# A transformer block with experts on one core: feed-forward output as three products of split operands, and the key epsilon as a product

## The reference

```python
def softmax_kernel(x, proj, is_query):
    xp = einsum('bhnd,md->bhnm', x * norm, proj)
    diag = sum(square(x), -1) * 0.5 * norm * norm
    stab = max(xp, -1) if is_query else max(xp, (-1, -2))
    return ratio * (exp(xp - diag - stab) + EPS_K)
...
k_sum = sum(kp, axis=2);  denom = einsum('bhnm,bhm->bhn', qp, k_sum)
ctx = einsum('bhnm,bhnd->bhmd', kp, v)
out = einsum('bhnm,bhmd->bhnd', qp, ctx) / denom[..., None]
x = layer_norm(video + out @ Wo.T + bo, g2, be2)
ff = relu(x @ W1.T + b1) @ W2.T + b2
return layer_norm(x + ff, g3, be3)
```

## Time and profile before

| | before |
|---|---|
| median of 3 runs | 865.91 us |
| profiled execution | 865.57 us |
| its span, first to last instruction | 863.8 us |
| PE busy (matmul) | 717.7 us |
| DVE busy | 610.2 us |
| ACT busy | 436.4 us |
| POOL busy | 358.0 us |

### The profile page before, as it was taken

How to read it: one execution, slowest core, us unless ns; L and a number is a source line. 1 busy time by engine, 2 the same in 40 slices (tenths; PEclk the granted TensorE clock), 3 DMA queues, 4 the chain that set the end, 5 groups by cost and what they waited for, 6 DMA issues and landing times.

```text
span 863.8 us, 15601 instructions
## 1 busy us (share of the span) xinstructions
PE 717.7 (83%) x5761; PEld 580.3 (67%) x5761; DVE 610.2 (71%) x1387; ACT 436.4 (51%) x668; POOL 358.0 (41%) x305
## 2 busy tenths in 40 slices
PE   4778999999999999999999969022469999999930
PEld 3737758768778778788687658021359999888830
DVE  4735837978978978978879664667837666776681
ACT  3544745846746646647557522054044445555461
POOL 4084234525417416515535352200135555555573
PEclk9769999999999999999999979555569999999975
DMA  8000010021021020030110111240043555566494
GB/s 233 2 24 3 2 49 2 1 74 51 2 74 49 24 80 17 24 98 0 49 50 2 65 35 49 74 154 0 7 141 77 130 139 144 146 142 165 123 242 104
DMA packets 51229, 61.51 MB, mean 71 GB/s; under 512 B 9328, under 2 KB 45424, under 8 KB 51184
## 3 DMA queue, kind: packets, MB, share of 16 engines
q1 hardware_dynamic: 42928, 46.98, 16.9%
q0 software_dynamic: 7296, 13.77, 8.2%
q10 hardware_dynamic: 960, 0.17, 0.1%
HBM read 39.80 MB, written 21.10 MB: 71 GB/s over the span
## 4 chain that ended last, share of the span: by engine, by line
PE 71%; DVE 12%; ACT 8%; issue 4%; POOL 3%; DMA 1%; POOLq 0%; ACTq 0%; DVEq 0%
PE pF L1460 11%; PE pX L1460 11%; PE pX L1767 10%; PE pF L1501 7%; PE pA L1460 5%; PE pX L1471 4%; PE pA L1511 4%; ACT kp L506 3%; PE pX L1437 3%; PE pA L1437 3%; PE pA L1452 3%; PE pX L1452 3%; ACT kp L510 2%; DVE qe L1178 2%; PE pX L1543 2%
## 5 line engine op out<-in xcount | busy, mean ns | idle before, releaser
L1501 PE MATMUL pF<-w,h 128*128 128x256 f32 x512 | 120.2, 382 | 0.0
L1501 PEld LDWEIGHTS pF<-w,h 128*128 128x128 f32 x512 | 93.9, 190 | 14.8 <-issue 3.4
L810 POOL DMA_INDIRECT kp<-row_scratch,idx_g x32 | 41.5, 1297 | 128.3 <-issue 67.9
L733 POOL TENSOR_SCALAR ve<-mv 128x4 f32<-128x4 f32 x40 | 9.2, 229 | 206.3 <-DVE mv L891 205.9
L642 ACT ACTIVATE h<-pX,b1cur 128x512 f32<-128x512 f32 x64 | 44.2, 690 | 87.0 <-DVE b1cur L1329 68.7
L1767 PE MATMUL pX<-w_lo,h_hi 128*128 128x256 f32 x256 | 73.2, 286 | 0.8 <-issue 0.8
L1767 PE MATMUL pX<-w_hi,h_lo 128*128 128x256 f32 x256 | 72.4, 283 | 0.0
L1767 PE MATMUL pX<-w_hi,h_hi 128*128 128x256 f32 x256 | 72.4, 283 | 0.0
L474 ACT ACTIVATE h<-pF,b1c 128x512 f32<-128x512 f32 x64 | 44.3, 692 | 40.2 <-PE pF L1460 40.2
L1285 DVE TENSOR_TENSOR h_lo<-h,h_hi 128x512 fp32r<-128x512 f32 x64 | 42.9, 690 | 30.6 <-ACT h_hi L634 30.6
L897 DVE TENSOR_SCALAR z<-z,mv,rstd 128x256 f32<-128x256 f32 x64 | 58.8, 980 | 7.1 <-POOL rstd L735 7.1
(11 more groups left out here) (312 smaller groups left out, 1979.6 us busy)
## 6 DMA issues: line engine op xcount, KB each, us to landing
kp<-fc1T SPq DMA_DIRECT2D x8, 1024.0 KB
w<-fc2T SPq DMA_DIRECT2D x8, 1024.0 KB
xin<-video SPq DMA_DIRECT2D x8, 512.0 KB, 3.7
x<-video SPq DMA_DIRECT2D x8, 512.0 KB, 4.5
out<-x SPq DMA_DIRECT2D x8, 512.0 KB, 2.9
acc_scratch<-xf SPq DMA_DIRECT2D x8, 512.0 KB, 3.0
row_scratch<-y SPq DMA_DIRECT2D x8, 512.0 KB, 3.0
kp<-acc_scratch SPq DMA_DIRECT2D x4, 512.0 KB, 5.6
```

The lines of the kernel that those rows point to most:

```text
L810: pool.indirect_dma_start(xg[:, g, :], None, row_d, bass.IndirectOffsetOnAxis(ap=idx_g[:, g:g + 1], axis=0)).then_inc(gathered, 16)
L1501: ins = nc.tensor.matmul(pF[m][:, half * D:(half + 1) * D], h[:, k, tok(2 * m + half)], w2[:, k, :], start=(k == 0), stop=(k == FC - 1))
```

## The change

1. Feed-forward output. `h` gets a high part `h_hi` (ScalarE copies, new `ff_hi`, two by two among the first four `relu`, then one behind each) and a low part `h_lo` (GpSimd subtracts, new `rest_of_hidden`, eight per batch). `w2` is split once in batch 0: `w2_hi` on ScalarE behind `cs_copy`, `w2_lo` on VectorE ahead of the head masks. `ff_out` makes three float32r products where it made one float32 product. The first call takes all `h_hi` products first and the `h_lo` products last.
2. Key epsilon. `eps_k` goes. The context product gets one more step, the sum of `v` over the tiles (`vsum`, two GpSimd additions) times a constant epsilon, and the sum of keys gets `N * EPS_K` as the bias of `cs_copy`.
3. Order and homes. GpSimd does the eight `rest_of_hidden` ahead of `xnb` and the key sums; scale and shift of `x2` move to the end of its body. `normed(3)` goes from VectorE to ScalarE (`z_norm`, ahead of `exp_q`), with a small product `nz` on VectorE; the other norms use `scalar_tensor_tensor` with the root as a broadcast second input in the place of `tensor_scalar`. VectorE's `ln1_stats` moves ahead of the sum `x1`, `add_ff(0)` behind the norms. The pieces of the last `ff_out` are cut at 4, 5, 7 in place of 4, 6, 7. Buffers share homes: `x2` with `r`, `aT_hi` with `qsq_hi`, `aT_lo` with `qsq_lo`, `cs`, `vsum` and `oT` inside `qe`; the expert loop's `w2e` and the second half of the last sums get homes of their own.

```diff
+            def ff_hi(f, n):
+                act.wait_ge(h_ready, f * FC + n + 1)
+                nc.scalar.activation(h_hi[:, n, :], h[:, n, :], ACT.Copy).then_inc(h_hi_ready, 1)
...
-            def eps_k(i, t):
-                act.wait_ge(ke_ready, i * TT + t + 1)
-                nc.scalar.activation(kp[:, t, :], kp[:, t, :], ACT.Identity, bias=epsk_c[:, 0:1]).then_inc(kp_ready, 1)
...
+            def z_norm(u):
+                act.wait_ge(ny_ready, 2 * u + 1)
+                for t in range(TT):
+                    ins = nc.scalar.activation(z[:, t, :], z[:, t, :], ACT.Identity, bias=nz[:, t:t + 1], scale=rstd[3][:, t:t + 1])
+                ins.then_inc(zf_ready, 1)
...
                 if ff:
                     for n in range(4, FC):
                         relu(f, n)
-                if att:
-                    for t in range(2):
-                        exp_k(i, t)
-                        eps_k(i, t)
+                        ff_hi(f, n)
+                if att:
+                    exp_k(i, 0)
+                    exp_k(i, 1)
                     q_tops(i)
...
+                if ut:
+                    z_norm(u)
...
+                    if isinstance(i, int) and i == 0:
+                        act.wait_ge(wff_in, 16 * N_WFF)
+                        nc.scalar.activation(w2_hi[:], w2[:], ACT.Copy).then_inc(w2_hi_ready, 1)
...
+            def rest_of_hidden(f, n):
+                pool.wait_ge(h_hi_ready, f * FC + n + 1)
+                nc.gpsimd.tensor_tensor(h_lo[:, n, :], h[:, n, :], h_hi[:, n, :].bitcast(F32), ALU.subtract).then_inc(h_lo_ready, 1)
...
+                if i is not None:
+                    pool.wait_ge(v_ready, (i + 1) * 2)
+                    nc.gpsimd.tensor_tensor(vsum, v[:, 0:2], v[:, 2:4], ALU.add).then_inc(vsum_ready, 1)
+                    pool.wait_ge(vsum_ready, 2 * i + 1)
+                    nc.gpsimd.tensor_tensor(vsum[:, 0], vsum[:, 0], vsum[:, 1], ALU.add).then_inc(vsum_ready, 1)
                 if f is not None:
-                    nc.gpsimd.tensor_tensor(x2[:], x2[:], g2_b[:]...
+                    for n in range(FC // 2):
+                        rest_of_hidden(f, n)
                 if u is not None:
                     root(3, u)
                 if f is not None:
-                    nc.gpsimd.tensor_tensor(x2[:], x2[:], b2_b[:]...
+                    for n in range(FC // 2, FC):
+                        rest_of_hidden(f, n)
...
+            def norm_tile(k, t, dst, src):
+                return nc.vector.scalar_tensor_tensor(out=dst[:, t, :], in0=src[:, t, :], scalar=mv[k][:, t, 0:1],
+                                                      in1=rstd[k][:, t:t + 1].to_broadcast([P, D]), op0=ALU.subtract, op1=ALU.mult)
...
+                if isinstance(i, int) and i == 0:
+                    dve.wait_ge(w2_hi_ready, 1)
+                    nc.vector.tensor_tensor(w2_lo[:], w2[:], w2_hi[:].bitcast(F32), ALU.subtract).then_inc(w2_ready, 1)
...
-                        ins = nc.tensor.matmul(pF[m][:, half * D:(half + 1) * D], h[:, k, tok(2 * m + half)], w2[:, k, :],
+                    if m == half == 0:
+                        for k in range(FC):
+                            pe.wait_ge(h_hi_ready, f * FC + k + 1)
+                            nc.tensor.matmul(dst, h_hi[:, k, rows], w2_lo[:, k, :], start=(k == 0), stop=False)
+                            nc.tensor.matmul(dst, h_hi[:, k, rows], w2_hi[:, k, :], start=False, stop=False)
+                        for k in range(FC):
+                            pe.wait_ge(h_lo_ready, f * FC + k + 1)
+                            ins = nc.tensor.matmul(dst, h_lo[:, k, rows], w2_hi[:, k, :], start=False, stop=(k == FC - 1))
+                    else:
+                        for k in range(k0, k1):
+                            for n, (h_, w_) in enumerate(((h_hi, w2_lo), (h_lo, w2_hi), (h_hi, w2_hi))):
...
-                        for t in range(TT):
+                        for t in range(TT + 1):
...
+                                w_, x_ = (v[:, t, cols], kp[:, t, tok(place_of(pair))]) if t < TT else (vsum[:, 0, cols], epsk_c[:, 0:1].to_broadcast([P, P]))
```

More of the change, by code:

```diff
@@ L30 @@
 EPS_K = 1e-4
-N_CONST = 14
+N_CONST = 15
 N_WFF = 13
-N_SEL = 9
+N_SEL = 8
 LN_EPS = 1e-5
@@ L128, in build @@
         w1_lo = sb("w1_lo", [P, C, FF], F32R)
-        w2 = sb("w2", [P, FC, D])
+        with ExitStack() as raw:
+            w2 = raw.enter_context(nc.sbuf_tensor("w2", [P, FC, D], F32))
+        w2_lo = sb("w2_lo", [P, FC, D], F32R)
+        w2_hi = sb("w2_hi", [P, FC, D], F32R)
         gate = sb("gate", [P, C, 32])
@@ L185, in build @@
         gT = sb("gT", [P, P])
-        h = sb("h", [P, FC, N])
+        with ExitStack() as raw:
+            h = raw.enter_context(nc.sbuf_tensor("h", [P, FC, N], F32))
+        h_lo = sb("h_lo", [P, FC, N], F32R)
+        h_hi = sb("h_hi", [P, FC, N], F32R)
         w1_raw = h[:].rearrange("p a b -> p (a b)")[:, 0:C * FF].rearrange("p (c n) -> p c n", c=C)
@@ L277, in build @@
             y = early("y", [P, TT, D])
-        h_hi, h_lo = (sb(n, [P, FC, N], F32R) for n in ("h_hi", "h_lo"))
-        w2_hi, w2_lo = (sb(n, [P, FC, D], F32R) for n in ("w2_hi", "w2_lo"))
-        h_f = h[:].rearrange("p a b -> p (a b)")
-        acc_s = [a.rearrange("p (k t d) -> p k t d", k=LQ, t=TT) for a in (kp_f, h_f)]
+        x2, aT_hi = r, qsq_hi
+        bv_wide = y[:].rearrange("p t d -> p (t d)")[:, 0:C * P].rearrange("p (c n) -> p c n", c=C)
+        w2e = sb("w2e", [P, FC, D])
+        b2cur = sb("b2cur", [P, D])
+        b1e = sb("b1e", [P, E, FC])
+        idm = sb("idm", [P, E, SR, GT])
+        idf = sb("idf", [P, E, GT])
+        Rbd = sb("Rbd", [P, 2, 4, SB], F16)
+        Rbd_be = Rbd[:].rearrange("p k e b -> p k b e")
+        acc_late = sb("acc_late", [P, LQ, TT, D])
+        acc_s = [kp_f.rearrange("p (k t d) -> p k t d", k=LQ, t=TT), acc_late[:]]
         sq_f = sq[:].rearrange("p a b d -> p (a b d)")
@@ L557, in body @@
                     squares(i, 0)
+                if ff:
+                    relu(f, 0)
+                if att:
                     squares(i, 1)
                 if ff:
-                    relu(f, 0)
                     relu(f, 1)
+                    ff_hi(f, 0)
+                    ff_hi(f, 1)
                 if att:
@@ L567, in body @@
                     relu(f, 3)
+                    ff_hi(f, 2)
+                    ff_hi(f, 3)
                 if att:
@@ L1047, in body @@
                 if u is not None:
-                    su.link(normed(3, u, z, z))
+                    dve.wait_ge(rstd_ready[3], u + 1)
+                    nc.vector.scalar_tensor_tensor(out=nz[:], in0=mv[3][:, :, 0], scalar=-1.0, in1=rstd[3][:], op0=ALU.mult,
+                                                   op1=ALU.mult).then_inc(ny_ready, 1)
+                if more:
+                    ln1_stats(i + 1)
+                if u is not None:
+                    dve.wait_ge(zf_ready, u + 1)
                     dve.wait_ge(xres_in, 16 * (u + 1))
@@ L1076, in heads_out @@
                                             rden[:, t, :].unsqueeze(2).to_broadcast([P, H, DH]), ALU.mult).then_inc(at_ready, 1)
-                if f is not None:
-                    add_ff(0)
                 if i is not None:
@@ L1092, in body @@
                     ln1_norm(i + 1)
+                if f is not None:
+                    add_ff(0)
                 if f is not None and i is None:
@@ L1113, in body @@
                     dve.wait_ge(xnb_ready, i + 1)
+                    if f is not None:
+                        dve.wait_ge(z_ready, 2 * (f + 1))
                     for m in range(2):
@@ L1687, in body @@
                     if ff:
-                        ff_out(1, 1, 4, 6)
+                        ff_out(1, 1, 4, 5)
                     pe.wait_ge(oT_ready, (i + 1) * 3)
-                    for t in range(TT):
-                        turn_out(t)
+                    turn_out(0)
+                    turn_out(1)
+                    if ff:
+                        ff_out(1, 1, 5, 7)
+                    turn_out(2)
+                    turn_out(3)
                 if gt_:
@@ L1695, in body @@
                 if att:
-                    if ff:
-                        ff_out(1, 1, 6, 7)
                     pe.wait_ge(at_ready, (i + 1) * TT)
```

110 lines of the change are left out of this document (51 added, 59 removed).

## The result

The changed kernel takes 905.72 us (median of 4 runs, 905.63 to 906.76), the kernel before 865.88 beside it (863.96 to 866.53): ratio 1.0467, interval 1.0449 to 1.0485. It is 40 us slower, where 14 were forecast.

The account below looks back on a forecast made before the run. The prediction took TensorE (PE) to bound the kernel, with the other engines close behind. From 865.57 us, +10.5 for seven bodies, +3.6 for batch 0 and 0 for the end gave 879.7, so 880; range 853 to 891.

Parts of the forecast that it names:

- part 4: Overlap of GpSimd's new work with VectorE's path: four `k_sub` wait 3.4 us a body; called the part that decides.
- the reading part: Share of a GpSimd operation, some 0.7, that a `k_sub` meeting it waits for; scaled from the `wo_lo` row.
- The rival of exclusion for the whole instruction: Each `k_sub` waits until GpSimd's instruction ends: +3.5 us a body, 894 us in all; chance 0.12.
- my +1.5: Net change per steady body: 2.7 + 0.47 - 0.29 - 1.42 = +1.5 us; seven bodies, +10.5 us.
- The drains: The end of the kernel, after the batch bodies: bounded between -2.8 and +2 us, taken as zero.
- one of my signs of being wrong: PE's longest new wait would be at the first `ff_out`, for `h_lo`, which the forecast had just in time.
- Query features: PE's start on them, released by VectorE's `rest_of_tops`, would come 2.7 us later in each body.
- Their second half: Query features' second half: the 2.7 us delay, +0.47 for epsilon products, -0.29 for the old fourth key tile wait.
- the forecast's -1.42: Saving per body from cheaper products in the last two `ff_out` calls: 1.42 us.
- Part 1: Float32r products in `ff_out`: 24 take 2.82 us for 3.53, saving 0.71 us a call, 2.84 us a body.
- Part 5: Batch 0: splitting `w2` ahead of the head masks delays them, +3.6 us, bounds 0 and 6.
- The first rival: No port between VectorE and GpSimd matters, PE is the path: -1.6 us a body, 858 us; chance 0.34.

Follow-up runs that it names:

- m1_port: Separate kernel, twelve stages, each one GpSimd operation chained beside one VectorE operation; two-input subtraction waited 0.94 of GpSimd's 1.26 us.
- c2_xf: Changed kernel with key bias in PSUM, W2's low part formed one body later, norm `xf` ahead of the head masks; 861.39 us (ratio 0.996).
- a2_kbias_psum: Changed kernel with the key bias in PSUM in place of SBUF, nothing else; 868.58 us (ratio 1.0043).
- e1_best: c2_xf with VectorE norms as tensor_scalar; in drains, norm of z on VectorE and scale and shift of `x2` ahead of `h_lo`; 859.18 us (ratio 0.994).
- e2_rest_only: e1_best with the key bias back in SBUF; 899.45 us (ratio 1.0372).
- m2_operands: Separate kernel, VectorE 128x256 operations alone, then beside GpSimd's 128x512 subtraction, copy or memset; tensor_scalar beside the memset took 1.00 us for 0.41.

## Why the prediction was wrong

**The direction was right, the size was not:** +40 us where +14 was forecast, above the range's end of 891. Mechanism and place (two-input `k_sub` against GpSimd's new work) were those of part 4.

**Part 4 failed at one step, "I take the reading part, some 0.7 of it".** A `k_sub` waits for GpSimd's instruction to its end. The waits were put at 0.3, 0.9, 0.7 and 1.5 us, 3.4 in all; they are 0.57, 1.10, 1.13 and 2.18, 4.98 in all. The rival of exclusion for the whole instruction had 0.5, 1.1, 1.1 and 2.3. The nearest row, `wo_lo`, showed 0.11 us beside a read of 128 columns, and I scaled that. It was misread, too: the GpSimd instruction began under `wv_lo` and ended at 14.18 + 0.45 = 14.63, and `wo_lo` at 14.34 + 0.80 = 15.14, 0.51 us later, which is its free 0.69 less 0.18. As far as so short a row can tell, it had waited to the other's end. And the 7.09 us norm, one piece for each GpSimd instruction, was the row of the right length and I gave it 0.12. The Trainium skill ("SBUF — State Buffer", Who interferes with whom) had the whole instruction; the trace agrees for these instructions, which have two inputs each, but for 0.13 to 0.14 us by which each of the four waits is shorter than what was left of the GpSimd instruction. Beside GpSimd's tensor_scalar m1_port shows less than the whole (0.8 of 2.84 us), and there the measurement decides.

**The rival had the waits right, but not the time.** It put +3.5 us on a body and 894 in all, and 905.7 was measured. Of the 3.7 us by which a body missed my +1.5, this step accounts for 1.6; 1.1 and 1.0 are two further waits, below, that neither forecast priced. The drains, set to nothing and measured at 8.4 us, are the other large part.

**The other terms of a body**, by PE's offsets from the turn of the key maxima in the two traces:
- `relu(4)` 1 us later and `hidden(6)` 0.5 us later (0.6 forecast): right.
- The first `ff_out`: I had `h_lo` just in time. PE waited 1.19 us for its last piece, since GpSimd is held by `k_sub` in its turn. This was one of my signs of being wrong, and it is as long as the longest other wait (1.18); but PE then waits 0.75 us more for VectorE's maxima, so it is not on the path.
- Query features: +4.3 us, where 2.7 was forecast. The 1.6 us between them are `k_sub`'s.
- Their second half: +5.6 where 2.9 was forecast (2.7 + 0.47 - 0.29). A further wait of 1.1 us, which I had not seen: ScalarE's norm of z stands ahead of its copy of the query features, and waits for `nz`, which waits for a key sum.
- The last two `ff_out`, up to the product of the heads: -0.9; the rest of the forecast's -1.42 falls behind the next item.
- `xf`: the wait of 1.0 us (1.1 with small gaps ahead of it). I had named it ("up to 2 us if the norms `xf` and `xn` have to wait for them") and set it to nothing; it was there in every steady body, and c2_xf removed it.
- The sum: 5.6 - 0.9 + 1.1, less about 0.5 behind it, from the last pieces of `ff_out` and from the old wait of 0.48 us for the turned heads, is the +5.2 a body that the trace has, in place of +1.5.

**The other parts.** Part 1's saving was right a product (0.12 us each, 2.9 us for 24), and in the change some 0.9 us a body of it came through, where the last two `ff_out` stand; the rest ended in waits. The context product takes 2.4 us, as forecast. Part 5 was put at +3.6 us: the masks came 4.9 later, 1.3 of it from before, and removing the step gave back 2.9. The drains were bounded by -2.8 and +2 and set to zero; the stretch from the last turn of the key maxima to the last statistics took 103.6 us, against 95.2 before. 5.3 of these 8.4 us are `k_sub`'s waits and their train in body 7 (a2_kbias_psum: 98.3 us, 464.07 to 562.37); the other 3.1 are steps of the drains that I had set to zero, and e1_best took back 0.8 us against c2_xf (98.6 to 97.8).

**The first rival ("no port between them matters", 858)** describes the kernel with its cause taken away: with the bias in PSUM and the two other waits (batch 0's masks, `xf`) gone, c2_xf has bodies of 60.05 us and 861.4 us. The change's saving was real; it was sold for a wait.

**What stays open:** which steps the 2.6 us are that the drains of e1_best still take over those of before; and how the 6 us between e2_rest_only and the change fall on its single repairs, none of which was run by itself with the bias in SBUF. In the two traces, 4.3 us apart, 2.2 us lie between the first two turns of the key maxima (batch 0, 64.57 against 66.76 us), 0.7 in the five steady bodies together, and none between the last turn and the last statistics (103.6 us in both). What decides whether the clock falls ahead of PE's long wait or behind it, no run here shows.

## What to carry to other kernels

Before work goes to GpSimd, list the VectorE instructions that will run beside it. One with two SBUF inputs, or a tensor_scalar or copy from SBUF to SBUF, pays nearly the whole length of each two-input GpSimd instruction in front of it, however short it is itself; one with an operand in PSUM, a reduction or the statistics paid nothing here. A small operand that is broadcast anyway may live in PSUM: for `k_sub` it cost nothing (1.213 against 1.217 us), and that one line was worth 37 us. Price every wait: the two that I had left at nothing cost more (2.1 us a body) than the one that I had mis-sized (1.6). And look at what a *removed* step had held back: without the epsilon piece a GpSimd sum got ahead of the instruction that it had followed.

## What the runs showed of the hardware that I had not expected

- A tensor_scalar with one tensor input waits for GpSimd as a two-input instruction does (1.30 us for 0.29 to 0.41), and for a memset too (1.00 us); PSUM at either end ends the wait for the subtraction (beside the memset it was not run). The Trainium skill ("SBUF — State Buffer", Who interferes with whom) has tensor_scalar and copy on its list by their fast mode over both port pairs; m2_operands agrees, and my expectation for m1_port had overlooked it.
- A two-input instruction that waited ends a little less than its free length behind the other's end: 1.09 us for 1.22 in the change (0.13 less, four times), 1.08 for 1.23 in m1_port (24.25 to 25.33).
- GpSimd's tensor_scalar holds VectorE for a part only: at 128x1024 it takes 2.84 us alone and made the two-input subtraction wait 0.8 (2.02 in place of 1.23), which then ended before it did. Its copy, which has one input as well, takes 1.04 us and cost 0.7 (1.94): most of its length, as with the two-input subtraction (0.94 of 1.26). Its memset (0.95 us) cost the two-input subtraction nothing (1.22 to 1.23).
